# Row maximum of the scores over blocks of 32 queries and 56 keys, on quarter columns and four banks a step, in a fused attention and ternary layer

## What is computed

```python
q, k, v = heads(ln(x) @ Wq.T + bq), heads(ln(x) @ Wk.T + bk), heads(ln(x) @ Wv.T + bv)   # 16 heads of 32
scores = q @ k.T / sqrt(32)
scores = where(delta < 0, -inf, scores) - delta          # delta = query position - key position
x = x + ln(softmax(scores) @ v @ Wo.T + bo)
xh = ln(x) @ hadamard                                    # 512 x 512
x = x + ln(quantize4(xh) @ ternary(weight).T)
```

## Time and profile before

| what | value |
|---|---|
| median of 3 runs | 1378.68 us (1378.66 to 1381.09) |
| the profiled execution | 1378.96 us |
| its span, first to last instruction | 1377.4 us |
| mean granted clock of PE | 0.985 |
| busy: PE, PEld, DVE, ACT, POOL | 94%, 61%, 73%, 46%, 41% |
| matmul and vector instructions | 17056 on PE, 2552 on DVE |

### The profile page before, as it was taken

One profiled execution on the slowest core, in us unless ns is written; L12 is line 12 of the kernel. 1 busy time (PEld: TensorE's weight loads), 2 busy tenths in 40 slices (PEclk: granted clock), 3 DMA queues, 4 the chain that ended last, 5 costly groups with the idle time before them and its releaser, 6 DMA issues.

```text
span 1377.4 us, 41217 instructions
## 1 busy us (share of the span) xinstructions
PE 1293.2 (94%) x17056; PEld 838.0 (61%) x17088; DVE 1001.2 (73%) x2552; ACT 627.0 (46%) x1395; POOL 566.7 (41%) x714
## 2 busy tenths in 40 slices
PE   3789999999999999999999999999999999999862
PEld 2566666666666666666666666666666666666430
DVE  4767777777777777777777778777777877777773
ACT  3244444544444444444444454544445454444441
POOL 1033444343444444344444444444443454443341
PEclk9899999999999999999999999999999999999996
DMA  8433443224344323334433233443323344322310
GB/s 244 92 79 93 109 108 95 76 81 108 79 109 109 94 75 86 105 79 109 109 94 83 78 106 78 109 109 94 86 82 98 78 109 109 94 71 67 83 47 18
DMA packets 69760, 128.58 MB, mean 93 GB/s; under 512 B 14880, under 2 KB 15648, under 8 KB 69472
## 3 DMA queue, kind: packets, MB, share of 16 engines
q1 hardware_dynamic: 64880, 108.84, 31.2%
q0 software_dynamic: 4688, 17.04, 3.3%
HBM read 41.43 MB, written 16.78 MB: 42 GB/s over the span
## 4 chain that ended last, share of the span: by engine, by line
PE 85%; DVE 5%; ACT 3%; issue 3%; SPq 1%; POOL 1%; DMA 1%; POOLq 0%; ACTq 0%; DVEq 0%
PE f_job L1013 48%; PE f_job L1170 8%; PE f_st L1117 5%; PE f_o L1137 4%; PE f_job L1188 4%; PE f_o L1142 4%; PE f_job L1085 3%; PE f_job L1042 3%; PE f_job L1097 2%; PE f_job L1161 2%; DVE f_x2Tl L817 1%; PE f_job L1178 1%; ACT f_PT L501 1%; SPq L314 1%; ACT f_x2Th L525 1%
## 5 line engine op out<-in xcount | busy, mean ns | idle before, releaser
L396 POOL TENSOR_TENSOR f_square<-f_stage 128x512 bf16<-128x512 f16 x128 | 130.7, 1042 | 260.8 <-ACT f_stage L479 260.8
L381 POOL TENSOR_SCALAR_AFFINE_SELECT f_PT<-f_PT 64x512 f32<-64x512 f32 (+1 forms) x256 | 164.3, 662 | 151.9 <-ACT f_PT L501 105.3
L387 POOL TENSOR_TENSOR f_OTl<-f_o,f_OTh 128x256 f16<-128x256 f32 x128 | 92.2, 721 | 273.6 <-ACT f_OTh L519 273.6
L479 ACT ACTIVATE f_stage<-f_job,f_bias 128x256 f16<-128x256 f32 x256 | 107.3, 470 | 169.8 <-PE f_job L1013 169.8
L732 DVE SCALAR_TENSOR_TENSOR f_stage<-f_job,f_bias,f_stage 128x256 f16<-128x256 f32 x256 | 111.6, 478 | 80.7 <-ACT f_stage L479 80.7
L501 ACT ACTIVATE f_PT<-f_st 128x512 f32<-128x512 f32 x192 | 108.4, 595 | 93.1 <-PE f_st L1117 93.1
L1013 PE MATMUL f_job<-f_xTh,f_wqh 128*128 128x256 f16 x512 | 141.0, 275 | 9.0 <-DVE f_wkl L630 5.9
L1013 PE MATMUL f_job<-f_xTh,f_wql 128*128 128x256 f16 x512 | 140.8, 275 | 0.0
L1013 PE MATMUL f_job<-f_xTl,f_wqh 128*128 128x256 f16 x512 | 140.8, 275 | 0.0
L1013 PE MATMUL f_job<-f_xTh,f_wkh 128*128 128x256 f16 x512 | 140.0, 273 | 0.0
L1013 PE MATMUL f_job<-f_xTh,f_wkl 128*128 128x256 f16 x512 | 139.9, 273 | 0.0
(11 more groups left out here) (155 smaller groups left out, 3184.7 us busy)
## 6 DMA issues: line engine op xcount, KB each, us to landing
f_stacks<-f_stage SPq DMA_DIRECT2D x384, 128.0 KB, 2.4
f_xin<-x SPq DMA_DIRECT2D x32, 512.0 KB, 5.1
f_xres<-x SPq DMA_DIRECT2D x32, 512.0 KB, 4.2
out<-f_z POOLq DMA_DIRECT2D x32, 512.0 KB, 3.4
f_Vmix<-f_V SPq DMA_DIRECT2D x32, 256.0 KB, 3.2
f_Vmix<-f_V SPq DMA_DIRECT2D x64, 128.0 KB, 3.3
f_stacks<-rows_const SPq DMA_DIRECT2D x3, 512.0 KB, 7.3
f_stacks<-wqT SPq DMA_DIRECT2D x1, 1024.0 KB, 9.5
```

The source lines that it names most:

```text
L381: nc.gpsimd.affine_select(out=d, in_=d, compare_op=ALU.is_ge, fill=0.0, base=odd * SUB, pattern=[[0, 4], [0, TP], [1, SUB]], channel_multi ...
L387: nc.gpsimd.tensor_tensor(OT[s % 2][1][:, g, :], o32[:, g % 2, :], OT[s % 2][0][:, g, :], ALU.subtract).then_inc(OTl_made, 1)
L396: nc.gpsimd.tensor_tensor(square[:, 2 * m + pair, :], h, h, ALU.mult).then_inc(squared, 1)
L479: nc.scalar.activation(stage[:, 2 * m, g, :], bank("qk", g)[:, m * W2:(m + 1) * W2], ACT.Identity, bias=bias[:, m, g:g + 1]).then_inc(qk_h ...
```

## The change

A unit now covers four heads: eight slots of 56 columns (`BW` = 24 + 32), in four blocks of 32 queries, each a matmul on 32 of PE's columns. So there are four units and four banks a step where there were eight, and a reduction reads 128 x 448 and gives 128 x 8. Each query's window reaches back as far beyond its block as before (24 keys), and the block itself is 32 instead of 64. A unit has 40 matmuls (36 in the first step of a sequence) where it had 12 (10). Together with this the order on each engine is written anew: `ORDER` has 24 places for 28, and calls have moved on PE, DVE, ACT and POOL.

```diff
-ORDER = (("qk", 0), ("max", 0), ("q", 0), ("qk", 1), ("q", 1), ("qk", 2), ("qk", 3), ("f", 0),
-         ("f", 1), ("y", 0), ("y", 1), ("v", 0), ("v", 1), ("s", 0), ("s", 1), ("turn", 0),
-         ("turn", 1), ("norms", 0), ("s", 2), ("s", 3), ("x", 0), ("h", 0), ("s", 4), ("s", 5),
-         ("s", 6), ("s", 7), ("x", 1), ("h", 1))
+ORDER = (("qk", 0), ("q", 0), ("max", 0), ("qk", 1), ("q", 1), ("qk", 2), ("qk", 3), ("f", 0),
+         ("f", 1), ("y", 0), ("y", 1), ("v", 0), ("v", 1), ("s", 0), ("turn", 0), ("s", 1),
+         ("norms", 0), ("turn", 1), ("s", 2), ("s", 3), ("x", 0), ("h", 0), ("x", 1), ("h", 1))
...
 BACKW = 24
-BW = BACKW + SUB
+ROWS = P // 4
+BW = BACKW + ROWS
+SLOTS = 8
...
             def maxima(n, i):
-                dve.wait_ge(scored, 8 * n + i + 1)
+                dve.wait_ge(scored, 4 * n + i + 1)
...
-                nc.vector.tensor_reduce(rmax[:, n % 2, 4 * i:4 * i + 4],
-                                        bank("s", i)[:, 0:4 * BW].rearrange("q (i k) -> q i k", k=BW),
+                nc.vector.tensor_reduce(rmax[:, n % 2, SLOTS * i:SLOTS * i + SLOTS],
+                                        bank("s", i)[:, 0:SLOTS * BW].rearrange("q (i k) -> q i k", k=BW),
                                         AX_X, ALU.max).then_inc(max_found, 1)
...
-                for sub in range(2):
-                    rows = slice(sub * SUB, (sub + 1) * SUB)
-                    pe.matmul(dst[rows, 0:4 * BW], identb[:, rows], window_sb[:, at0:at0 + 4 * BW],
+                for sub in range(4):
+                    rows = slice(sub * ROWS, (sub + 1) * ROWS)
+                    pe.matmul(dst[rows, 0:SLOTS * BW], identb[:, rows], window_sb[:, at0:at0 + SLOTS * BW],
                               start=True, stop=False)
-                for slot in range(4):
-                    h, I = 2 * i + slot // 2, slot % 2
-                    for sub in range(2):
+                for slot in range(SLOTS):
+                    h, I = SLOTS // TP * i + slot // TP, slot % TP
+                    for sub in range(4):
...
                         mm = pe.matmul(dst[rows, slot * BW + lo:(slot + 1) * BW], queries,
-                                       Ks[n % 3][0:RP, h, q0 - BACKW + lo:q0 + SUB],
-                                       start=False, stop=(slot == 3))
+                                       Ks[n % 3][0:RP, h, q0 - BACKW + lo:q0 + ROWS],
+                                       start=False, stop=(slot == SLOTS - 1))
```

More of the change, by code:

```diff
@@ L411, in _ @@
                     square_of(n, 0)
+                if has(k):
+                    heads_low(k, 3)
                 if has(m):
                     front_root(m)
-                if has(k):
-                    heads_low(k, 3)
                 if has(s):
@@ L554, in _ @@
                 n, m, k = s + 1, s + 2, s - 1
-                if s == -1:
-                    weights_high(2)
+                if has(s):
+                    keep_max(s)
                 if has(n):
@@ L559, in _ @@
                 if s == -1:
[L560 to L564, removed]
+                    weights_high(2)
                 if has(k - 1):
@@ L616, in _ @@
                     front_high(m, 1)
+                if has(k):
+                    round_levels(k, 0)
                 if has(s):
@@ L923, in _ @@
                     keep_norms(n)
+                    maxima(n, 1)
+                if s == -1:
+                    weights_low(3)
                 if has(k):
                     x2_low(k, 1)
+                if has(n):
+                    maxima(n, 2)
+                if has(s):
+                    normalise(s, 2)
+                if has(n):
+                    maxima(n, 3)
                 if s == -1:
                     fold_bias()
-                if has(n):
-                    maxima(n, 2)
-                    maxima(n, 3)
-                if has(s):
-                    normalise(s, 2)
                 if has(k):
@@ L947, in _ @@
                     level(k, 0)
+                if has(n):
+                    split_max(n)
             gs = [0]
@@ L1197, in _ @@
                     qk(n, 0)
+                if has(k - 1):
+                    turn_q(k - 1, 0)
                 if has(s):
                     turn_max(s)
[L1200 to L1201 removed]
                 if has(n):
@@ L1232, in _ @@
                     scores(n, 0)
-                    scores(n, 1)
-                if has(s):
-                    keys(s, 3, 0)
                 if has(k):
                     turn_x2(k, 0)
-                if has(s):
-                    keys(s, 3, 1)
+                if has(n):
+                    scores(n, 1)
+                    norms(n)
                 if has(k):
@@ L1243, in _ @@
                     turn_tern()
-                if has(n):
-                    norms(n)
                 if has(s):
+                    keys(s, 3, 0)
+                    keys(s, 3, 1)
                     weigh(s, 2)
@@ L1801 @@
     at = np.arange(BW)[None, :] - BACKW
-    window = np.where(at <= il % SUB, (at - il % SUB) * SS, LOW)
-    window = np.tile(window, (1, 7))
-    for slot in (0, 2):
-        window[:SUB, slot * BW:slot * BW + BACKW] = LOW
+    window = np.where(at <= il % ROWS, (at - il % ROWS) * SS, LOW)
+    window = np.tile(window, (1, 2 * SLOTS - 1))
+    for slot in range(0, SLOTS, TP):
+        window[:ROWS, slot * BW:slot * BW + BACKW] = LOW
     tok = np.arange(W2)
```

56 lines of the change are left out of this document (18 added, 38 removed).

## The result

| what | before | changed |
|---|---|---|
| median of the runs | 1378.67 us (1378.21 to 1381.09) | 1360.38 us (1356.21 to 1363.62) |
| ratio of the runs, with its 95% interval | | 0.9862 (0.9826 to 0.9898) |
| the profiled execution, its span | 1378.96, 1377.4 us | 1356.21, 1354.7 us |
| mean granted clock of PE | 0.985 | 0.984 |

The change gains some 18 us (22.7 between the two profiled executions), where 43 were forecast. 1360 lies inside the range of 1319 to 1364.

What follows compares the result with a forecast made beforehand. TensorE's own queue of work, busy for 94% of the span, was taken as the bound. 1.32 us saved a step gives 41 us over 31 stretches, plus 2 at the start: 1378.96 − 43 = 1336 us, range 1319 to 1364.

Steps and rivals of the forecast that it cites:

- Part 1: Row-maximum units on TensorE: four new units take 1.82 us a step where eight took 2.68.
- the bound of the issue price: Upper bound for a unit's 40 matmuls on TensorE: 14 ns each, thus 0.56 us a unit.
- The size of a unit: Ordinary unit of 40 matmuls on TensorE: 0.455 us, bounded by 0.373 and 0.56.
- Part 2: TensorE's new order, first unit to next projection: 10.64 us against 12.28, from units, two waits and tile changes.
- Part 3: Who answers late: VectorE loaded 9.63 us of 10.64, 91%; 0.3 us charged in two kinds of step.
- The two waits of 0.1 to 0.2 us: TensorE waits for the fourth unit's bank, about 0.1 us, and before the next projection, 0.1 to 0.2.
- rival A: Late VectorE answers take the gain back: 0.64 us a step left of 1.32, 1357 us; chance 0.22.
- The cover of the restacking transfers: Restacking transfers may start 0.7 us late, covered by 4.3 us less landing before the next first unit.
- Part 4: Start and end: 2 us gained from TensorE's waits in the start, within 0 to 4; last steps have no units.
- Rival B: Quarters on TensorE run as two pairs, a unit takes 0.75 us: 1363 us; chance 0.05.
- Rival C: Unit matmuls paid by the piece, 28 ns each, a unit 1.12 us: 32 us slower, 1411 us; chance 0.10.

Runs made afterwards that it cites:

- e4: The burst: changed kernel with 512 idle matmuls of 56 columns ahead of the first unit of step 7; 1373.77 us, one run.
- e8: Changed kernel with 1011 matmuls of 512 columns split in two, putting the 256-instruction boundary 90 behind the third weighing's start; 1346.39 us, 0.9739 of the kernel before.
- run 27: Not a run: the words are part of "long-run 27", the 27 ns a matmul in the long run, measured with 512 idle matmuls in the changed kernel.
- e7: The changed kernel run once more, nothing altered; 1362.24 us, 0.9854 of the kernel before.
- e10: The changed kernel run once more on another chip, nothing altered; 1364.74 us, 0.9864 of the kernel before.
- e5: Changed kernel with fulfilled waits among each step's projections, putting the 256-instruction boundary 90 behind the third weighing's start; 1490.81 us, 1.0810 of the kernel before.

## Why the prediction was wrong, and where it was right

**The step that failed: Part 1, the bound of the issue price, and with it the sum, which has no term for bringing the instructions in.** It took "as an issue price, by the densest row in quarter tiles", 14 ns a record, for the upper bound of what a matmul costs. That row has eight records, and the norms and weighings around it eat few instructions; it shows the price while the supply lasts, not the price at which the supply renews itself. The burst gives both: 11.5 ns within a piece of 128 matmuls and 27 ns over many. The change put 4096 instructions more into the list, and the third and fourth unit are now a cluster of 160. What their supply costs was put at nothing: it is 17.0 us in the stretches of the profiled execution. The count closes: 15 ordinary stretches, 7 without earlier keys and 7 behind those save 15 × 1.40 + 7 × 1.36 + 7 × 1.11 = 38.3 us undisturbed; less 17.0, and less 1.2 by which the steps outside the stretches grew, that is 20.1, and the two kernels drift 20.3 us apart from the first of these stretches (122.21 us before, 120.78 now) to the one behind the last (1283.98, 1262.26). With e8, which takes nearly all the holes away, the gain over before is 35.3 us on its chip. The forecast's 43, less some 2 for the splits, 4 for the waits for the stacks, 2 for the two holes left and 1 for the start, are 34.

**The size of a unit** was 0.455 us in the forecast and is 0.50: two units with a change of tile (0.09) take 636.67 − 635.58 = 1.09 us. That lies within the bounds (0.373 to 0.56), 0.05 × 4 × 31 = 6 us too little.

**The order** (Part 2) came out. Its sum was 10.64 without waits; with units of 0.50 it is 10.82, and 10.88 was measured. Per four steps the undisturbed stretches save 2 × 1.40 + 1.36 + 1.11 = 5.27 us, where 5.29 were forecast. That the two agree so well is luck in part: the units were 0.18 a step too cheap and the waits 0.3 too dear.

**VectorE** (Part 3): the reduction takes 0.617 us (0.62 forecast), 128 of them, and the load is 9.47 us of 10.88, 87% for 91%. The two waits of 0.1 to 0.2 us don't appear; TensorE is busy for all of the 10.88. So rival A, waits that take the gain back, did not come. Its group on the page:

```profile
L744 DVE TENSOR_REDUCE f_rmax<-f_job 128x8 f32<-128x448 f32 x128 | 78.9, 617 | 25.4 <-PE f_job L1090 24.7
```

The cover of the restacking transfers was misjudged there too: "4.3 us less landing cover it" left the landing unpriced. e8's waiting step shows it at 3.8 us, so of the 4.3 some half a microsecond was left (other steps need less: in the changed kernel the issues end at 666.48 and the unit starts at 669.84 without a wait).

**The start** (Part 4): the first projection of step 1 begins at 60.83 us for 61.92, 1.1 us gained for 2; the split of the front (L720) is still awaited there.

**Rival B**, pairs of quarters one after the other, is excluded by units of 0.50 us. **Rival C** named the right place, and that the number of matmuls counts and not only what they stream; it got 10 in 100. Its mechanism, one price for every matmul, is refuted by units of 0.50 us. That its 28 ns stand near the supply's long-run 27 is a coincidence as far as the runs show: it was read from a unit of twelve, in which no hole was seen. A piece of 256 instructions stands ready, so that a cluster of 80 or 160 is mostly paid only if the boundary falls in it. The time came out between forecast and C. It lies in the range, next to A's 1357, but for a reason that no case of the prediction has: that is luck, not a hit.

The Trainium skill, TensorEngine Tiling (Array Packing), section Instruction Overhead, states about 60 cycles a matmul, by estimate 25 ns. The runs disagree within a piece, at 11.5 ns for a matmul of 56 columns; the 27 ns over many are near its figure, but are paid in holes after each 128th matmul, not by each one.

## What to carry to other kernels

Count the instructions of a change, not only their durations: on TensorE a cluster of many short matmuls was paid at 6 ns an instruction out of what is at hand, and at 13.5 ns where piece after piece of 256 had to be brought in. When a profile shows idle time "by issue" that recurs at some steps and not at others with the same work, number the engine's list modulo 256 before looking for a wait. If the holes fall on one number, move the boundary into work that streams long, by splitting or joining large matmuls there; here it cost some 2 us of matmuls and was worth as much as the change itself.

## What the runs showed of the hardware

- TensorE's instructions come in pieces of 256, a packet of 16 KB on queue 8 each. In the changed kernel it takes 2.2 to 2.9 us from the start of the packet to the first matmul of the piece, where TensorE waits for it. In the burst a new piece comes every 3.45 us (e4); in the changed kernel the two packets that follow each other most closely while it works start 3.3 us apart.
- The boundary has a fixed place in the program: every hole of these steps, in all kernels whose list I numbered, ended at 194 modulo 256.
- A packet can come later by some 2 us without a change of the program, and then a hole stands where there usually is none (e7, e8, e10).
- A fulfilled wait is no free filler: 34 to 82 instructions of them cost 1.1 to 6.6 us a step, each further one at a place some 0.11 us (e5).
- The burst left a trace of its own: TensorE was idle for more than half of 316 to 331 us, the granted clock fell to 0.62 there and was 0.80 on the mean of the next 14 us. At the lower level, 1.2 GHz, the four transposes that take 0.66 us elsewhere are recorded with 1.12. Windows of e4:

```profile
316.00:331.00 15.00, 6.92 (x518) 6.01 (x520) 0.56 (x2) 0.60 (x1) 1.11 (x2) 0.62 0.17 42
331.00:345.00 14.00, 14.00 (x309) 9.14 (x299) 10.14 (x23) 6.33 (x14) 3.27 (x5) 0.80 0.02 4
345.00:356.00 11.00, 11.00 (x117) 9.56 (x117) 6.76 (x21) 5.70 (x13) 3.59 (x5) 1.00 0.32 98
```

Open stay why a fulfilled wait in e5 costs what it does, what makes a packet come late, and whether the kernel before, whose units take 28 ns a matmul, would gain from an alignment. It shows no such hole; nothing of this was tried.
